# Four message-passing layers on one core: empty gather columns left out, the segment softmax with one exchange each way, and the back pass of layer 2 moved on VectorE

## The reference, cut to what matters

```python
# layer 1: a gate per edge, two segment sums
src_diff = segment_sum(h_src - h_dst, dst)
h_diff = segment_sum(src_diff[src] * gate, dst)
out = relu(h_diff @ W_ffn.T + b_ffn)
# layer 2: attention with one head over the edges of each dst
att = leaky_relu(a, 0.01)
expv = exp(att - segment_max(att, dst)[dst])
w = expv / segment_sum(expv, dst)[dst]
out = segment_sum(w[:, None] * (z_src + ez), dst)
# layer 3: the same with four heads, and with a loop at every node
alpha = ex / (segment_sum(ex, dst)[dst] + 1e-16)
out = segment_sum(x[src] * alpha[:, :, None], dst).mean(axis=1) + bias
# layer 4: a small network on every edge, and its maximum per node
out = segment_max(relu(concat([x_i, x_j - x_i]) @ W1 + b1) @ W2 + b2, dst)
```

## Time and profile before

| block | from, to (us) | length | DVE busy | POOL busy | PE busy |
|---|---|---|---|---|---|
| setup | 0 to 56.2 | 56.2 | 22.08 | 42.05 | 3.86 |
| stage A | 56.2 to 606.9 | 550.7 | 413.79 | 387.54 | 210.68 |
| layer 1 | 615.0 to 902.9 | 287.9 | 191.54 | 205.35 | 178.22 |
| layer 2, nodes and logits | 902.9 to 1237.8 | 334.9 | 285.37 | 208.92 | 270.00 |
| softmax of layer 2 | 1247.1 to 1277.0 | 29.9 | 17.29 | 0.00 | 3.38 |
| layer 2, messages | 1277.0 to 1474.0 | 197.0 | 157.24 | 0.00 | 126.72 |
| layer 3, nodes and logits | 1474.0 to 1756.7 | 282.7 | 243.16 | 205.89 | 189.59 |
| softmax of layer 3 | 1756.7 to 1826.8 | 70.1 | 46.13 | 0.00 | 3.40 |
| layer 3, messages | 1826.8 to 2095.5 | 268.7 | 218.53 | 0.00 | 221.66 |
| layer 4 | 2095.5 to 2643.7 | 548.2 | 280.49 | 415.07 | 180.76 |

### The profile page before, as it was taken

The page is one execution under the profiler, slowest core; times in us unless marked ns, Lnnn a source line. Parts: engine busy times, 40 slices in busy tenths (PEclk is TensorE's granted clock), DMA queues, the critical chain, the costliest instruction groups (busy, mean ns, idle before and its releaser), DMA issues. The chain is left out here.

```text
span 2643.7 us, 25893 instructions
## 1 busy us (share of the span) xinstructions
PE 1391.6 (53%) x5742; PEld 830.5 (31%) x5742; DVE 1886.1 (71%) x3916; ACT 792.9 (30%) x1636; POOL 1466.0 (55%) x1409
## 2 busy tenths in 40 slices
PE   1433433334666588886566577633888543333331
PEld 1332333332333344443233454411333222121110
DVE  4877777775777589997688699966888666464542
ACT  0322222222555355654111355521222110010100
POOL 7777777745777576661000577720000277777776
PEclk9655556566877799998688799965889666566666
DMA  4433333331111233332011244420000110101010
GB/s 162 124 107 106 108 107 107 107 84 35 48 48 48 58 101 110 107 106 58 20 38 38 82 130 127 128 63 11 30 26 30 27 22 24 24 23 24 22 22 12
DMA packets 118512, 175.58 MB, mean 66 GB/s; under 512 B 36928, under 2 KB 43182, under 8 KB 118324
## 3 DMA queue, kind: packets, MB, share of 16 engines
q1 hardware_dynamic: 72052, 129.98, 14.7%
q0 software_dynamic: 44800, 44.60, 9.0%
q10 hardware_dynamic: 1600, 0.33, 0.1%
HBM read 89.27 MB, written 86.87 MB: 67 GB/s over the span
## 5 line engine op out<-in xcount | busy, mean ns | idle before, releaser
L447 POOL DMA_INDIRECT GA<-table,look_i x600 | 620.2, 1034 | 509.6 <-PEq L1440 230.1
L1596 POOL DMA_INDIRECT GA<-table,look_i x200 | 205.1, 1025 | 414.3 <-PEq L1670 353.6
L453 PE MATMUL P<-ident,GA 128*128 128x128 f32 x500 | 104.3, 345 | 451.5 <-DMA GB<-in_x,dst_i 213.7
L477 PE MATMUL P<-center,work 128*128 128x128 f32 x800 | 154.1, 355 | 210.7 <-DVE work L1662 175.0
L253 POOL DMA_INDIRECT GA<-in_x,src_i x200 | 217.5, 1087 | 80.4 <-issue 72.2
L1604 POOL DMA_INDIRECT out_x<-work,seg_i x200 | 210.0, 1050 | 61.0 <-issue 60.6
L253 POOL DMA_INDIRECT GB<-in_x,dst_i x200 | 200.8, 1004 | 61.0 <-issue 61.0
L453 PEld LDWEIGHTS P<-ident,GA 128*128 128x128 f32 x500 | 70.4, 174 | 481.8 <-issue 229.7
L495 ACT ACTIVATE work<-P 128x512 f32<-128x512 f32 x100 | 59.8, 598 | 516.4 <-PE P L477 516.3
L477 PEld LDWEIGHTS P<-center,work 128*128 128x128 f32 x800 | 137.5, 259 | 242.3 <-issue 113.7
L596 PE MATMUL P<-center,work 128*128 128x128 f32 x984 | 159.3, 311 | 94.3 <-ACT work L639 68.6
(11 more groups left out here) (320 smaller groups left out, 3454.7 us busy)
## 6 DMA issues: line engine op xcount, KB each, us to landing
table<-work SPq DMA_DIRECT2D x175, 256.0 KB, 2.4
XN<-in_x SPq DMA_DIRECT2D x98, 256.0 KB, 2.7
out_x<-work SPq DMA_DIRECT2D x98, 256.0 KB, 2.1
GA<-table,look_i POOLq DMA_INDIRECT x800
XN<-in_src_pad SPq DMA_DIRECT2D x13, 512.0 KB
cols<-in_dst_pad SPq DMA_DIRECT2D x50, 128.5 KB
table<-XD SPq DMA_DIRECT2D x1, 6400.0 KB
src_wide<-in_src_pad SPq DMA_DIRECT2D x12, 512.0 KB, 5.0
```

The costliest lines, as they stand in the source:

```text
L447: pool.indirect_dma_start(GA[:, par, j * D:(j + 1) * D], None, table_k, bass.IndirectOffsetOnAxis(ap=look[:, s * 8 + j:s * 8 + j + 1], axis=0)
L453: ins = pe.transpose(dst[:, q * 128:(q + 1) * 128], src[:, q * 128:(q + 1) * 128], ident[:, :])
L477: ins = pe.matmul(norm_bank(par, far)[:, q * 128:(q + 1) * 128], W[par][4][:, q * 128:(q + 1) * 128], center[:, :], start=True, stop=True)
L1596: pool.indirect_dma_start(GA[:, par, j * D:(j + 1) * D], None, table[3], bass.IndirectOffsetOnAxis(ap=look_i[:, r * 8 + j:r * 8 + j + 1], ...
```

## The change

1. `filled(s)` names the places j of a tile that hold an edge: all eight, but 0, 2, 4 and 6 in the last tile. Gathers and scatters are issued for these alone, and the waits for the last tile count `LACK` = 64 less (twice that in stage A). In layer 4, where the last tile comes first, POOL first sets the gather buffer of parity 0 to zero.
2. The zero half of table 0 is written from one 128x512 tile (`XN[:, 0, :]`) that is read 25 times, in place of 128x12800 of `XD`; POOL's memset shrinks to 128x512.
3. `softmax_rows` scans upward and downward over the same source in one round. The maximum of the two is the segment's maximum; their sum less the source is the segment's sum. The downward scan of the maximum uses a new mask, `row_low`. There are two rounds, each with one exchange that carries both directions. The flags whether a whole row belongs to one segment (`runs`, `run_rows`) are worked out once, in the softmax of layer 2, before its logits are waited for. Within `every` the scans are not linked to each other. Loads and stores are one DMA for all heads, and each part of the weights is stored when it is ready. ACT's exponential starts before the subtraction for the own loops.
4. In layer 2's message stage `back_dve` yields step 3 in place of 1.

```diff
+        def filled(s):
+            return [j for j in range(8) if s * SE + j % 2 * HW + j // 2 * 128 < E]
+        LACK = 16 * (8 - len(filled(NS - 1)))
+        def landed(s, k, passes=1):
+            return k * 128 * passes - (LACK * passes if isinstance(s, int) and s == NS - 1 else 0)
...
-                for j in range(8):
+                for j in filled(s):
...
-                sp.dma_start(table[0][EP:2 * EP, :].rearrange("(p c) f -> p (c f)", p=128), XD[:, :]).then_inc(S("init"), 16)
+                sp.dma_start(table[0][EP:2 * EP, :].rearrange("(s p j) f -> p s (j f)", p=128, j=8),
+                             XN[:, 0:1, :].to_broadcast([128, NS, HW])).then_inc(S("init"), 16)
...
-                pool.memset(XD[:, :], 0.0).then_inc(S("fill"), 1)
+                pool.memset(XN[:, 0, :], 0.0).then_inc(S("fill"), 1)
...
-        def back_dve(dve, T, s, par, k):
-            yield 1
+        def back_dve(dve, T, s, par, k, step=1):
+            yield step
...
-                    for h in range(K):
-                        sp.dma_start(t[:, h, :], logits[lo + h, :].rearrange("(p c) -> p c", p=128)).then_inc(S("load"), 16)
-                sp.wait_ge(S("weights"), 1)
+                    sp.dma_start(t, by_head(logits[lo:lo + K, :])).then_inc(S("load"), 16)
                 for part in range(PARTS):
-                    for h in range(K):
-                        sp.dma_start(weights[part * K + h, :].rearrange("(p c) -> p c", p=128),
-                                     half[part][:, h * RC:(h + 1) * RC]).then_inc(S("store"), 16)
+                    sp.wait_ge(S("weights"), part + 1)
+                    sp.dma_start(by_head(weights[part * K:(part + 1) * K, :]),
+                                 half[part].rearrange("p (h c) -> p h c", h=K)).then_inc(S("store"), 16)
...
+                def scans(src, up, down, up_mask, down_mask, op0, op1, start, r):
+                    def every(begin_up, begin_down):
+                        for h in range(K):
+                            dve.tensor_tensor_scan(up[:, h, :], up_mask[:, :], src[:, h, :], begin_up(h), op0, op1)
+                        for h in range(K):
+                            ins = dve.tensor_tensor_scan(down[:, h, ::-1], down_mask[:, ::-1], src[:, h, ::-1], begin_down(h), op0, op1)
+                        link(ins)
+                    every(lambda h: start, lambda h: start)
+                    dve.tensor_copy(ends[:, 0:K], up[:, :, RC - 1])
+                    link(dve.tensor_copy(ends[:, HEADS:HEADS + K], down[:, :, 0]))
+                    dve.nop().then_inc(S("ends"), 1)
+                    dve.memset(up_in[:, 0:1], start)
+                    link(dve.memset(down_in[:, 128:129], start))
+                    dve.wait_ge(S("ends_row"), r)
...
+                    dve.nop().then_inc(S("carry"), 1)
+                    dve.wait_ge(S("carry_in"), r)
+                    link(dve.tensor_copy(carry_in[:, 0:2 * K], P[1][:, 0:2 * K]))
+                    every(lambda h: carry_in[:, h:h + 1], lambda h: carry_in[:, K + h:K + h + 1])
...
-                scan(L, T, row_neg, A.add, A.max, -BIG)
-                spread(T, R)
+                scans(L, T, R, row_neg, row_low, A.add, A.max, -BIG, 1)
+                link(dve.tensor_tensor(R, R, T, A.max))
...
-                scan(X, T, row_same, A.mult, A.add, 0.0)
-                spread(T, R)
+                scans(X, T, R, row_same, row_more, A.mult, A.add, 0.0, 2)
+                link(dve.tensor_tensor(T, T, X, A.subtract))
+                link(dve.tensor_tensor(R, R, T, A.add))
...
-                pipelined(dve, S3, None, message, summed, partial(norm_dve, dve), partial(back_dve, dve))
+                pipelined(dve, S3, None, message, summed, partial(norm_dve, dve), partial(back_dve, dve, step=3))
...
+                pool.memset(GA[:, 0, :], 0.0).then_inc(S6("pads"), 1)
+                pool.wait_ge(S6("pads"), 1)
```

More of the change, by code:

```diff
@@ L755, in link, with whole_runs @@
                     dve.wait_ge(S("dve"), step[0])
[L757 to L767, removed]
+                def whole_runs():
+                    for i, mask in enumerate((row_neg, row_low, row_same, row_more)):
+                        link(dve.tensor_reduce(red[:, i:i + 1], mask[:, :], AX, A.min))
+                        link(dve.tensor_copy(runs[:, i * HEADS:(i + 1) * HEADS], red[:, i:i + 1].to_broadcast([128, HEADS])))
@@ L768, in scan @@
                     dve.nop().then_inc(S("ends"), 1)
+                    dve.memset(up_in[:, 0:1], start)
+                    link(dve.memset(down_in[:, 128:129], start))
                     dve.wait_ge(S("ends_row"), r)
[L770 to L773, removed]
+                    flags = run_rows[0:K, 256 * (r - 1):256 * r]
@@ L774, in scan @@
+                    dve.tensor_tensor_scan(up_in[:, 1:129], flags[:, 0:128], P[0][0:K, 0:128], start, op0, op1)
+                    link(dve.tensor_tensor_scan(down_in[:, 127::-1], flags[:, 255:127:-1], P[0][0:K, 255:127:-1], start, op0, op1))
                     dve.nop().then_inc(S("carry"), 1)
                     dve.wait_ge(S("carry_in"), r)
-                    link(dve.tensor_copy(carry_in[:, 0:K], P[1][:, 0:K]))
-                    for h in range(K):
-                        link(dve.tensor_tensor_scan(d(dst[:, h, :]), d(mask[:, :]), d(src[:, h, :]), carry_in[:, h:h + 1], op0, op1))
@@ L780, in spread @@
[L780 to L785, removed]
+                    link(dve.tensor_copy(carry_in[:, 0:2 * K], P[1][:, 0:2 * K]))
+                    every(lambda h: carry_in[:, h:h + 1], lambda h: carry_in[:, K + h:K + h + 1])
+                if not own:
+                    link(dve.tensor_scalar(row_low[:, :], row_more[:, :], -1.0, BIG, A.add, A.mult))
+                    whole_runs()
+                    dve.nop().then_inc(S("runs"), 1)
+                    dve.wait_ge(S("run_rows"), 1)
+                    link(dve.tensor_copy(run_rows, P[2][0:HEADS, :]))
@@ L818, in _ @@
                 if own:
-                    act.activation(XO, LO, ACT.Exp).then_inc(S("exp"), 1)
+                    act.wait_ge(S("own_shifted"), 1)
+                    act.activation(XO, LO, ACT.Exp).then_inc(S("own_exp"), 1)
             @block.tensor
             def _(pe):
-                for r, down in enumerate((False, True, False, True)):
+                if not own:
+                    pe.wait_ge(S("runs"), 1)
+                    for i in range(4):
+                        ins = pe.transpose(P[2][0:HEADS, 128 * i:128 * i + 128], runs[:, HEADS * i:HEADS * (i + 1)], ident[:, :])
+                    ins.then_inc(S("run_rows"), 1)
+                for r in range(2):
                     pe.wait_ge(S("ends"), r + 1)
-                    pe.transpose(P[0][0:K, 0:128], ends[:, 0:K], ident[:, :])
-                    pe.transpose(P[0][0:K, 128:256], ends[:, HEADS:HEADS + K], ident[:, :]).then_inc(S("ends_row"), 1)
+                    for i in range(2):
+                        ins = pe.transpose(P[0][0:K, 128 * i:128 * i + 128], ends[:, HEADS * i:HEADS * i + K], ident[:, :])
+                    ins.then_inc(S("ends_row"), 1)
                     pe.wait_ge(S("carry"), r + 1)
-                    src = carry[0:K, 257:385] if down else carry[0:K, 256:384]
-                    pe.transpose(P[1][:, 0:K], src, ident[0:K, 0:K]).then_inc(S("carry_in"), 1)
+                    pe.transpose(P[1][:, 0:K], up_in[:, 0:128], ident[0:K, 0:K])
+                    pe.transpose(P[1][:, K:2 * K], down_in[:, 1:129], ident[0:K, 0:K]).then_inc(S("carry_in"), 1)
         with nc.Block() as block:
@@ L1594, in gather @@
                     pool.wait_ge(S6(f"slot_free{par}"), s // 2 + 1)
-                    for j in range(8):
+                    for j in filled(r):
                         pool.indirect_dma_start(GA[:, par, j * D:(j + 1) * D], None, table[3],
@@ L1664, in _ @@
                 pipelined(dve, S6, back, stream, lambda T, s, par, k: norm_dve(
[L1665 removed]
+                    dve, T, s, par, k, "scattered", 0 if isinstance(s, int) and s < 2 else 128 * (k - 1) - (LACK if par == 0 else 0)), unrolled=True)
             @block.tensor
```

36 lines of the change are left out of this document (22 added, 14 removed).

## The result

The changed kernel took 2575.75 us (median of four runs, 2573.75 to 2577.51) and the kernel before 2644.1 (four runs, 2642.62 to 2645.9): a ratio of 0.9741 with a 95% interval of 0.9724 to 0.9758. Forecast were 2581 and 2567 to 2597. The spans of the two profiled executions, 2643.7 and 2575.7, differ by 68.0 us, against the forecast's 62.

What follows compares the result with a forecast made beforehand. By block, DVE bounds layer 2's message stage, POOL layer 4, POOL's last gathers setup and tile ends, DVE chains the softmaxes. Terms sum to -62 on 2645.48 us: 2583.5, or 2581 against the runs' median; range 2567 to 2597.

Steps and rivals of the forecast that it cites:

- Setup: Setup block: the minimum is held by POOL's memset; shrinking the memset brings gathers earlier, 6.9 us off (4.5 to 7.3).
- the zero DMA: In setup: with 2 KB rows at 296 GB/s it takes 22.1 us and ends at 49.3.
- Ends of tiles: Last tiles with fewer gathers: stage A 4.95 us, layer 1 3.1, layer 3's nodes and logits 3.0, layer 2's 0.
- stage A: Eight gathers fewer save POOL 10 us, but DVE, ending the block, idled only 4.95: gain 4.95 (0 to 10).
- Layer 4: Four gathers and four scatters fewer save 10.7 us, the new memset costs 0.9: gain 9.8 (9 to 10.7).
- The message stage: Layer 2: the back pass fills DVE's wait for ACT's root, 0.44 us a slot over 23 slots: 9.7 gained.
- Rival C: Layer 2's message stage is not DVE's: PE and ACT take up the 0.44, 9.7 us stay, 2591; chance 0.06.
- The softmaxes: Softmax of layer 3 17.9 us shorter and of layer 2 6.6 shorter, from rounds, loads, stores and small steps.
- two rounds in place of two pairs: Layer 3's softmax: a round of 11.0 us replaces an up-and-down pair of 17.71, twice: -13.4 (-10 to -16).
- the loads: Layer 3's softmax: 12 load DMAs become 3, -1.4 us (0 to -1.9).
- the stores: Layer 3's softmax: two of three parts are stored while DVE makes the next, -4.4 us.
- The scan's start-to-start: Softmaxes: unlinked scans taken at 0.50 us, 0.55 with a carry, between bounds 0.43 to 0.60 and 0.49 to 0.66.

Runs made afterwards that it cites:

- the experiment that stores behind the last part: Changed kernel with half the old memset added, scans linked again, and weights stored only when the last part is ready; 2591.39 us in one run.
- part 4 alone: Kernel before with only the back pass of layer 2's message stage moved behind the sum of squares; 2628.66 us, ratio 0.996.
- the other form of the minimum: Kernel before with only setup's minimum written as a scalar_tensor_tensor in place of a tensor_scalar; 2637.79 us in one run.
- part 2 or 3 alone: Kernel before with only the small memset and repeated-tile zero DMA (ratio 0.9987), or with only the one-round softmax (ratio 0.9922, 2619.83 us).
- the four parts alone: Four kernels, each the kernel before with one numbered part of the change; ratios 0.9912, 0.9987, 0.9922 and 0.996 for parts 1 to 4.

## Why the prediction was right

**Setup.** The mechanism held: the memset held the minimum, and both go. The landing of the last gather came where it was put, 47.6 against "near 48". Mis-sized was the step from there to the block's end: "I take 6.9 off" sets the end to 56.2 - 6.9 = 49.3, the time worked out for the end of the zero DMA, and leaves nothing for POOL's drain and the barrier behind it. From the last landing to the block's end they take 2.5 us before and 2.9 after. Another error went the other way and hid about half of it: 22.1 us for the zero DMA by the stores' 296 GB/s was too slow, 20.3 were measured. So setup gave 5.7 in place of 6.9.

**Ends of tiles.** Layer 1 and layer 3 came out at -3.0 and -2.9 against 3.1 and 3.0, and layer 2's nodes and logits, where PE does not wait for the last gathers, at -0.4 against 0. So the right reading was to count not POOL's earlier finish but the idle time of the engine that ends the block. In stage A the same reading gives, over the profiles: the last gather starts 12.5 us earlier from the block's start, and from there to the block's end it takes 41.6 in place of 36.0, so 6.9 remain. Of the 12.5, 10.3 lie in the last tile itself, from its first gather to its last (19.5 us with sixteen, 9.2 with eight); they alone leave 4.7, near the forecast's 4.95. The other 2.2 are already there before the last tile's first gather. Stage A differs by up to 5.1 between profiles of the same code, roughly in step with the mean time of one gather (1.043 us where it took 547.25, 1.062 where it took 551.11), so they are not shown to be the change's.

**Layer 4** was too small by 2.9. The memset, put at 0.9, costs 0.25: POOL issued its first gather only 0.74 us after the barrier before, and 0.99 now, so most of it lies in a stretch that was there anyway. From the end of POOL's last scatter to the end of the kernel there are 10.1 us in place of 10.75, in every profile with 392 DMAs against every one with 400. The difference is in POOL's last drain, 8.55 against 9.20, which starts only when the last scatter has landed; why it is shorter is open. The rest, about 1.5, comes from a slightly smaller mean time of one DMA with its gap (1.334 to 1.341 against 1.341 to 1.344), and was not tried apart.

**The message stage** gave 10.4, the upper end of the step's 9.2 to 10.1 and a little more. Rival C would have needed PE or ACT to take the 0.44 us a slot; the single wait that is left shows that neither did, and DVE's other waits for PE and ACT in this stage come to 10.1 us against 9.9 before.

**The softmaxes** came out by their terms: two rounds in place of two pairs -14.0 against -13.4, the loads -1.55 against -1.4 (barrier to first operation 7.48, now 5.93), the stores -4.2 against -4.4 (last part to barrier 7.64, now 3.48). Of these 4.2, the 2.8 of the experiment that stores behind the last part come from storing early; the rest would be the fewer DMAs, which were not tried apart. The scan's start-to-start, which no row had, is 0.47 and 0.53, between the bounds 0.43 to 0.60 and 0.49 to 0.66, nearer the lower ends and a little under the 0.50 to 0.55 that were taken.

**Not foreseen**: layer 3's message stage is 2.2 longer. No part touches it. It took 268.6 to 268.8 in the kernel before, with part 4 alone and with the other form of the minimum, and 270.7 to 271.8 in the six other profiles, part 2 or 3 alone among them. What it depends on stays open. It is part of why the four parts alone add up to less than the whole (0.88 + 0.13 + 0.78 + 0.40 = 2.19% against 2.59%, or 10.6 us less): three of them carry 2.0 to 2.8 us each, the changed kernel once, which makes 5 of the 10.6. The rest is not explained; by the spans of the single profiles the parts add up to more than the whole, 77.1 against 68.0 us, so such sums tell little.

## What to carry to other kernels

Where barriers cut a program into blocks, forecast block by block and take, for an engine that finishes earlier, only the idle time of the engine that ends the block. A wait on an engine is worth its length only where that engine sets the pace: the same 9.2 us of waiting were worth 10 in one stage and nothing that stands out of the spread in another. An operation whose duration ends with another engine's may be held and not slow; the same arithmetic in another form tells which, for the price of one line.

## What the runs showed of the hardware

A DVE tensor_scalar on 128x200 int32 was held from its start to 0.1 us past the end of a GpSimd memset that only writes, with 10.76 us and with 5.42 us of memset; a scalar_tensor_tensor with two inputs ran beside it in 0.37. A semaphore of DVE on itself between two scans of 128x200 cost 0.13 us each. Writing 6,400 KB of zeros in rows of 2 KB from one repeated tile took 1.4 us longer than in rows of 51 KB, and in rows of 10 KB 0.5 longer. POOL's drain behind its gathers ended 1.6 to 2.4 us after the last of them had landed in the profiles looked at, and the one at the kernel's end took 9.20 us after 400 DMAs and 8.55 after 392.
